# Softmax steps of equal width in a fused adaLN, attention and expert kernel: key blocks 7 and 1, 6 and 2, 5 and 3 share a score bank

## The reference

```python
h = layernorm(x) * (1 + ca) + sa
# attention: 16 heads of size 8, rotary embedding (the odd half of each pair becomes 0), causal
scores = where(causal, Q @ K^T / sqrt(8), -1e10);  y = softmax(scores) @ V
x = x + ga * (y @ Wo^T + bo)
h = layernorm(x) * (1 + cb) + sb
# experts: h @ Wm + bm is cut into 8 slices of 16; each slice takes its best 2 of 16 experts,
# gelu(t @ W1[e] + b1[e]) @ W2[e] + b2[e], weighted by the softmax over the 16 logits
x = x + gb * (experts(h) @ Wo2 + bo2)
```

## Time and profile before

| what | us |
|---|---|
| time, median of 3 runs (lowest, highest) | 398.37 (398.05, 399.06) |
| time of the profiled execution | 399.35 |
| its span | 397.5 |
| TensorE busy | 339.4 (85%) |
| VectorE busy | 287.7 (72%) |
| ScalarE busy | 256.8 (65%) |
| GpSimd busy | 134.2 (34%) |
| ScalarE exponentials and Gelus (L770), 225 instructions | 198.5 |

### The profile page before, as it was taken

How to read it: one execution, slowest core, us unless ns; L and a number is a source line. 1 busy time by engine, 2 the same in 40 slices (tenths; PEclk the granted TensorE clock), 3 DMA queues, 4 the chain that set the end, 5 groups by cost and what they waited for, 6 DMA issues and landing times.

```text
span 397.5 us, 7269 instructions
## 1 busy us (share of the span) xinstructions
PE 339.4 (85%) x2637; PEld 158.0 (40%) x2668; DVE 287.7 (72%) x590; ACT 256.8 (65%) x297; POOL 134.2 (34%) x175
## 2 busy tenths in 40 slices
PE   3659687888798599988998899988899898879996
PEld 3425244545464344433644444433554323132123
DVE  5879868997889957787489677876569546973334
ACT  7570443535178658874558878864567997968981
POOL 6246207201302604672110624742204025532500
PEclk9957789999999979999999999999999999999999
DMA  7334123200026045540116155530123255815550
GB/s 272 94 68 77 41 43 54 42 1 3 4 49 98 17 123 133 143 102 7 31 37 101 54 137 133 148 62 3 30 39 42 82 137 144 125 47 138 151 135 26
DMA packets 27115, 31.53 MB, mean 79 GB/s; under 512 B 6780, under 2 KB 17788, under 8 KB 27068
## 3 DMA queue, kind: packets, MB, share of 16 engines
q1 hardware_dynamic: 23372, 28.57, 31.2%
q0 software_dynamic: 3456, 2.39, 2.9%
q10 hardware_dynamic: 252, 0.11, 0.2%
HBM read 3.57 MB, written 1.05 MB: 12 GB/s over the span
## 4 chain that ended last, share of the span: by engine, by line
PE 55%; DVE 21%; issue 8%; ACT 6%; DMA 4%; POOL 3%; SPq 2%; DVEq 0%; ACTq 0%; POOLq 0%
PE misc L1294 18%; PE acc L1294 18%; PE big L1294 17%; DVE mx L1032 8%; ACT ring L770 5%; PE misc L1316 2%; DMA block<-qk_turned 1%; DMA tstack<-tp 1%; SPq L517 1%; DMA cc<-in_pack_c 1%; SPq L492 1%; POOL block L446 1%; POOL gm L670 1%; DVE xn L976 1%; DVE gm L1152 1%
## 5 line engine op out<-in xcount | busy, mean ns | idle before, releaser
L770 ACT ACTIVATE ring<-big 128x1024 f32<-128x1024 f32 (+2 forms) x225 | 198.5, 928 | 94.5 <-PE big L1294 93.3
L1032 DVE TENSOR_REDUCE mx<-misc 128x1 f32<-128x512 f32 (+7 forms) x155 | 87.9, 588 | 25.1 <-PE misc L1294 23.1
L1294 PE MATMUL acc<-ring,cb 128*32 128x512 f32 x512 | 68.3, 609 | 1.5 <-DVE gm L1152 1.5
L1294 PE MATMUL big<-dense,block 128*128 128x448 bf16 (+7 forms) x249 | 54.2, 317 | 5.8 <-ACT ring L770 5.6
L1294 PE MATMUL big<-tstack,w1s 128*128 128x512 bf16 x178 | 53.0, 387 | 4.8 <-ACT ring L770 3.1
L1294 PE MATMUL misc<-dense,block 128*128 128x320 bf16 (+7 forms) x167 | 42.6, 318 | 8.7 <-DVE mx L1032 8.3
L1152 DVE SCALAR_TENSOR_TENSOR gm<-acc,cb,gm 128x512 f32<-128x512 f32 (+1 forms) x41 | 30.0, 733 | 24.5 <-PE acc L1294 19.4
L446 POOL DMA_DIRECT2D block<-qk_turned x66 | 39.4, 601 | 21.6 <-DMA tstack<-tp 20.7
L1294 PEld LDWEIGHTS big<-dense,block 128*128 128x128 bf16 x256 | 30.8, 149 | 30.7 <-ACT ring L770 16.0
L1294 PE MATMUL acc<-ring,vals 128*32 128x64 f32 (+7 forms) x512 | 40.1, 414 | 0.4
L1294 PEld LDWEIGHTS misc<-dense,block 128*128 128x128 bf16 x170 | 21.0, 150 | 48.3 <-DVE mx L1032 39.2
(11 more groups left out here) (163 smaller groups left out, 459.9 us busy)
## 6 DMA issues: line engine op xcount, KB each, us to landing
gm<-wT SPq DMA_DIRECT2D x64, 256.0 KB
dense<-qk SPq DMA_DIRECT2D x42, 64.0 KB
tstack<-tp SPq DMA_DIRECT2D x18, 128.0 KB, 4.4
block<-qk_turned POOLq DMA_DIRECT2D x66, 32.0 KB, 3.2
xs<-in_x SPq DMA_DIRECT2D x4, 256.0 KB, 8.0
ca<-in_pack_a SPq DMA_DIRECT2D x1, 769.0 KB, 7.7
out<-lg SPq DMA_DIRECT2D x3, 256.0 KB, 2.3
dense<-tp SPq DMA_DIRECT2D x6, 128.0 KB, 8.9
```

The source lines that it names most:

```text
L770: act.activation(dst, src, func, scale=scale).then_inc(s["ring_read"], 1)
L1032: dve.tensor_reduce(mx[:, g, k:k + n, blk], src, AX.X, ALU.max).then_inc(s["misc_read"], 1)
L1294: return pe.matmul(dst, lhsT, rhs, start=start, stop=stop)
```

## The change

The key blocks are taken in five steps: 0; 7 and 1; 6 and 2; 5 and 3; 4. In a step of two blocks one bank holds both blocks of one pair, 64 + 448 or 128 + 384 or 192 + 320 = 512 columns, and one masking matmul serves both diagonals. A group has 9 units instead of 12, each of exactly 1024 columns, so each exponential takes 128x1024. A step is weighed once the scores of the step two later are issued, one step at a time. 18 units per softmax are no multiple of the ring's 8 slots, so slots are counted from the start of the program. The points to which other work is tied move with it: on TensorE `turn_residual`, `tokens`, `logits`, `sums_out`; on ScalarE the three turns to units 8, 9, 10, the sums to 14, the logits' exponential to 15; in softmax 0 the woven work of VectorE. The loops of `softmax` on TensorE (L1415) change as `slots` does below.

```diff
--- before.py
+++ after.py
@@ -77,10 +77,22 @@
              for n in [min(GP, T // (BLK * (s + 1)))] for k in range(0, GP, n)]
 
 
-SCORE_UNITS = [(s, 2 * k, 2, 1) for s in range(4) for k in range(2)] + [
-    (4, 0, GP, 2), (5, 0, GP, 2), (6, 0, GP, GP), (7, 0, GP, GP)]
+SOFT_STEPS = [(0,), (7, 1), (6, 2), (5, 3), (4,)]
+NSS = len(SOFT_STEPS)
+
+
+def banks_of(step):
+
+    if len(step) == 1 and T - BLK * step[0] == T // 2:
+        return [[(k + j, step[0], j * T // 2) for j in range(2)] for k in range(0, GP, 2)]
+    return [[(k, blk, sum(T - BLK * x for x in step[:j])) for j, blk in enumerate(step)] for k in range(GP)]
+
+
+SCORE_UNITS = [(i, banks_of(step)[k:k + 2]) for i, step in enumerate(SOFT_STEPS) for k in range(0, len(banks_of(step)), 2)]
 NU = len(SCORE_UNITS)
-TURN_AT, SUM_AT, ROUTE_AT = (11, 12, 13), 18, 20
+HOME = {(k, blk): (u, T * bank + at) for u, (_, banks) in enumerate(SCORE_UNITS)
+        for bank, items in enumerate(banks) for k, blk, at in items}
+TURN_AT, SUM_AT, ROUTE_AT = (8, 9, 10), 14, 15
 EARLY = 4
 
 SHARED = NB - 1
...
@@ -125,12 +137,11 @@
     order = [("early", k) for k in range(2)]
     late = []
     for g in range(NG):
-        for blk in range(NS):
-            order += [("scores", g, u) for u in range(NU) if SCORE_UNITS[u][0] == blk and (g or u >= EARLY)]
-            if len(late) == 2:
-                order += late
-                late = []
-            late.append(("weigh", g, blk))
+        for i in range(NSS):
+            order += [("scores", g, u) for u in range(NU) if SCORE_UNITS[u][0] == i and (g or u >= EARLY)]
+            late.append(("weigh", g, i))
+            if len(late) > 2:
+                order.append(late.pop(0))
     return order
 
 
@@ -139,9 +150,8 @@
     if slot[0] == "early":
         return sum(columns_of(("scores", 0, u)) for u in range(EARLY // 2 * slot[1], EARLY // 2 * (slot[1] + 1)))
     if slot[0] == "scores":
-        blk, _, n, _ = SCORE_UNITS[slot[2]]
-        return n * (T - BLK * blk)
-    return 4 * (T - BLK * slot[2])
+        return 2 * T
+    return GP * sum(T - BLK * blk for blk in SOFT_STEPS[slot[2]])
 
 
 def woven():
@@ -181,7 +191,7 @@
     return uses, banks, previous, [last[1], last[3]]
 
 
-FOLD_AT, CUT_AT = [12, 15], [18, 21, 24, 27]
+FOLD_AT, CUT_AT = [8, 10], [12, 14, 16, 18]
 OPENING, OPENING_BANK, OPENING_PREVIOUS, LAST_IN_ACC = opening()
 
 
...
@@ -784,15 +794,13 @@
                 for u in range(SOFT):
                     if u in between:
                         between[u]()
-                    blk, _, n, per = SCORE_UNITS[u % NU]
-                    w = per * (T - BLK * blk)
-                    src = big[:, 2 * (u % 2):2 * (u % 2) + n // per, 0:w]
-                    dst = ring[:, u % RING, 0:w * (n // per)].rearrange("p (k w) -> p k w", w=w)
+                    src = big[:, 2 * (u % 2):2 * (u % 2) + 2, :]
+                    dst = ring[:, (phase[0] + u) % RING, :].rearrange("p (k w) -> p k w", k=2)
                     transform("softmax", phase, u, src, dst, ACT.Exp, SCALE)
 
             def take_sums(phase, groups=range(NG)):
                 for g in groups:
-                    wait_consumed(act, phase, NS * g + NS - 1)
+                    wait_consumed(act, phase, NSS * g + NSS - 1)
                     act.copy(sums[g][:, :], acc[:, g, :]).then_inc(s["acc_read"], 1)
 
             def route(here):
@@ -816,7 +824,7 @@
                     if u in between:
                         between[u]()
                     src = big[:, 2 * (u % 2):2 * (u % 2) + 2, :]
-                    dst = ring[:, u % RING, :].rearrange("p (k w) -> p k w", k=2)
+                    dst = ring[:, (phase[0] + u) % RING, :].rearrange("p (k w) -> p k w", k=2)
                     if b == NB - 1 and u == EXPERT - 1:
                         for k in range(2):
                             transform("experts", phase, u, src[:, k], dst[:, k], ACT.Gelu, 1.0)
...
@@ -1367,34 +1375,33 @@
             def scores(m, phase, u):
 
                 g = u // NU
-                blk, k0, n, per = SCORE_UNITS[u % NU]
-                w, at = T - BLK * blk, BLK * blk
                 pe.wait_ge(s["ring_read"], phase[0] + u + 1)
-                for bk in range(n // per):
-                    dst = big[:, 2 * (u % 2) + bk, 0:per * w]
-                    for j in range(per):
-                        p = GP * g + k0 + per * bk + j
-                        matmul(dst[:, w * j:w * j + w], blocks(k_block_of[m], p, blk), q_dense_of[m][:, p, at:T], start=(j == 0), stop=False)
-                    diagonals = dst.rearrange("p (n w) -> p n w", w=w)[:, :, 0:BLK]
+                for bank, items in enumerate(SCORE_UNITS[u % NU][1]):
+                    dst = big[:, 2 * (u % 2) + bank, :]
+                    for j, (k, blk, at) in enumerate(items):
+                        p, w = GP * g + k, T - BLK * blk
+                        matmul(dst[:, at:at + w], blocks(k_block_of[m], p, blk), q_dense_of[m][:, p, BLK * blk:T], start=(j == 0), stop=False)
+                    n, apart = len(items), items[-1][2] or BLK
+                    diagonals = dst[:, 0:n * apart].rearrange("p (n w) -> p n w", w=apart)[:, :, 0:BLK]
                     ins = matmul(diagonals, identb[:, :],
-                                 earlier_query[:, :].unsqueeze(1).to_broadcast([P, per, BLK]), start=False)
+                                 earlier_query[:, :].unsqueeze(1).to_broadcast([P, n, BLK]), start=False)
                 ins.then_inc(s["ring_filled"], 1)
 
-            def weigh(m, phase, g, blk):
-
-                units = [u for u in range(NU) if SCORE_UNITS[u][0] == blk]
-                pe.wait_ge(s["ring_read"], phase[0] + g * NU + units[-1] + 1 + CREDIT["ring_read"])
-                w = T - BLK * blk
-                if g == 0 and blk == 0 and m < len(LAST_IN_ACC):
+            def weigh(m, phase, g, i):
+
+                last = max(u for u in range(NU) if SCORE_UNITS[u][0] == i)
+                pe.wait_ge(s["ring_read"], phase[0] + g * NU + last + 1 + CREDIT["ring_read"])
+                if g == 0 and i == 0 and m < len(LAST_IN_ACC):
                     pe.wait_ge(s["misc_read"], LAST_IN_ACC[m] + 1 + CREDIT["misc_read"])
-                if blk == 0 and phase[2]:
+                if i == 0 and phase[2]:
                     pe.wait_ge(s["acc_read"], NG * m)
                     wait_taken(pe, m - 1, g - 2)
-                for k in range(GP):
-                    u = next(x for x in units if SCORE_UNITS[x][1] <= k < SCORE_UNITS[x][1] + SCORE_UNITS[x][2])
-                    at = (k - SCORE_UNITS[u][1]) * w
-                    ins = matmul(acc[VW * k:VW * k + VW, g, BLK * blk:T], vals[:, GP * g + k, blk, :],
-                                 ring[:, (g * NU + u) % RING, at:at + w], start=(blk == 0), stop=(blk == NS - 1))
+                for blk in SOFT_STEPS[i]:
+                    for k in range(GP):
+                        u, at = HOME[k, blk]
+                        ins = matmul(acc[VW * k:VW * k + VW, g, BLK * blk:T], vals[:, GP * g + k, blk, :],
+                                     ring[:, (phase[0] + g * NU + u) % RING, at:at + T - BLK * blk],
+                                     start=(i == 0), stop=(i == NSS - 1))
                 ins.then_inc(s["consumed"], 1)
 
             def sums_out(here, m, g):
...
@@ -1487,7 +1493,7 @@
                 wait_taken(pe, b, n - 2)
                 for e in range(EH):
                     ins = matmul(acc[HR * e:HR * e + HR, n % 2, :], w2[:, EH * half + e, :],
-                                 ring[:, (u0 + e) % RING, T * k:T * k + T])
+                                 ring[:, (phase[0] + u0 + e) % RING, T * k:T * k + T])
                 ins.then_inc(s["consumed"], 1)
 
             def combine(here, k, half, part="", cols=slice(0, T)):
@@ -1636,16 +1642,16 @@
 
                 softmax(b + 1, softmax_at(None, b), {
                     ("scores", 0, EARLY): first_links, ("scores", 0, EARLY + 1): lambda: project(here),
-                    (0, 5): lambda: turn_residual(here, 2 * b + 3),
-                    (0, 6): lambda: tokens(here), ("scores", 1, 1): lambda: logits(here),
-                    (1, 5): lambda: sums_out(here, b + 1, 0)})
+                    (0, 4): lambda: turn_residual(here, 2 * b + 3),
+                    (1, 0): lambda: tokens(here), ("scores", 1, 3): lambda: logits(here),
+                    (1, 3): lambda: sums_out(here, b + 1, 0)})
                 experts(here, experts_at(b), NG * b + 2 * NG, ahead=True, next_sums=b + 1)
             here = ("late", NB - 2)
             turn_output(here)
             softmax(NB - 1, softmax_at(NB - 1), {
-                ("scores", 0, EARLY): lambda: project_out(here), (0, 6): lambda: turn_residual(here, 2 * NB - 2),
-                ("scores", 1, 0): lambda: tokens(here), (1, 0): lambda: logits(here),
-                (1, 5): lambda: sums_out(here, NB - 1, 0)})
```

(38 more changed lines are left out.)

## The result

The changed kernel takes 399.74 us (median of 20 runs, 398.66 to 403.27), the one before 398.28 in the same session (20 runs). The ratio is 1.0044, 95% interval 1.0029 to 1.0059: slower by 1.2 to 2.3 us. The profiled execution took 400.1 us, with a span of 398.2 against 397.5 before.

What follows compares the result with a forecast made beforehand. TensorE, with over half the chain of waits, was taken as the bound, VectorE in softmax 0. Terms -0.5 + 0.75 - 1.05 - 0.7 + 1.7 = +0.2 us gave 398.6 us on the median's scale, range 395.3 to 400.9.

Steps and rivals of the forecast that it cites:

- (a): ScalarE's exponentials and Gelus: 201 records instead of 225, all 1024 wide but for the last unit's two halves.
- (e): End of softmax 0: VectorE's wait for the values above 1.9 us.
- (b): `tokens` after the last maximum: about 1.35 us later in softmax 2, 0.75 later in softmax 1, 0.65 earlier in softmax 3.
- (c): TensorE waiting 2 to 3.5 us before `routed` in experts 1 and 2, Gelu's table load beside the last weighing.
- Softmax 0, -0.5: Softmax 0: VectorE stays the bound, its small idle times shrink, its values wait grows; -0.5 us, bounds -1.5 and +1.5.
- Softmax 1, +0.75: Softmax 1 and handover to experts 0: later `tokens` delays the SyncE-GpSimd chain whole; +0.75 us, bounds 0 and +1.5.
- Softmax 2, -1.05: Softmax 2 and handover to experts 1: `tokens` later, but waits for ScalarE go; -1.05 us, bounds -2 and +1.35.
- Softmax 3, -0.7: Softmax 3: `tokens` and the chain through `route` start earlier, so `routed` does too; -0.7 us, bounds -1.5 and +0.5.
- The clock, +1.7: Before experts 2: TensorE's 3.4 us idling brings one fall to half clock; +1.7 us, bounds 0 and 2.5.
- two falls: The wait before experts 1 also brings a clock fall; 400.3 us, up to 400.9; chance 0.21.
- `route` does not bind: Softmax 2 and 3 gain TensorE's saved waits whole, 2.0 us each, softmax 1's tokens not late; 394 us, chance 0.12.

Runs made afterwards that it cites:

- experiment 4: VectorE's routing without the order among equal second-best values: on the changed kernel 393.58 us, ratio to before 0.9892; on the kernel before 397.17 us, ratio 0.9979.

## Why the prediction was right or wrong

The time fell inside the range, 1.1 us above the forecast. It is clear of noise on the slower side, to which I had given 0.27, the least of the three. The main mechanism was right: ScalarE's gain is worth nothing by itself, TensorE's saved waits stop at VectorE's route, and one long wait brings a fall of the clock. That the total came out this near is partly luck: softmax 1 and the count of falls were too low, the price of the fall was too high.

- **Signs (a) to (e)** came, but for sizes in (b) and (c): 201 exponentials and Gelus; tokens +1.39 in softmax 2 (said 1.35) and 0.64 earlier in softmax 3 (said 0.65), but +1.12 in softmax 1 (said 0.75); waits of 2.51 and 3.71 us before `routed` (said 2.3 and 3.4, and at most 3.5); half clock behind the latter; 2.10 us before the values. The experts' stage that holds no fall kept its length (A1 to Z1 39.71).
- **Softmax 0, -0.5**: too large. The first two profiles show -0.94, but with the clock at half speed until 50.0 instead of 52.2 us. Over five profiles with the old steps V lies at 92.96 on average, over seven with the new ones at 92.81: -0.15, less than its own scatter of 1 us.
- **Softmax 1, +0.75**: +1.12 (V to T1 23.97 with no fall, against 22.85). The late parts of the queries don't play in there, but the same extra wait for tokens (2.41 instead of 1.30) does, and its +1.35 of softmax 2 should have been the centre.
- **Softmax 2, -1.05**: -0.74. **Softmax 3, -0.7**: -0.68.
- **The clock, +1.7**: the fall came, at 1.03 us. I had priced it by the thin stretch up to the first product; there it is free, since that product waits for a DMA, and what is paid is the backlog behind it. For experts 0 the same method was too low (2.7).
- **The step that was off** is the count of falls. I counted the one place where the change makes a wait longest and took all else as equal. These terms alone give -0.15 + 1.12 - 0.74 - 0.68 + 1.03 = +0.6 us; measured are 1.6 on the means. Time at half clock elsewhere has the size of the missing us: the changed kernel has 8.5 us more of it on average, of which the fall before experts 2 is 3.4, and the other 5.1 at 0.22 are 1.1 us. That is an estimate from averages. The profiles do not show where the 5.1 lie. Of the changed kernel's two, both fell at 101 us (V to T1 24.78 and 24.93 against 23.97 without a fall) and one before `routed` in experts 1 (0.74); of the kernel before's two, neither fell at 101, but one at 212.6 (1.6). Over all profiles the fall at 101 stands in five of eight with the new steps and in two of five with the old, and in those two it lasts 6.9 us instead of 3.4 and costs 1.9 us (V to T1 24.79 and 24.80 against 22.85), in the five 0.6 to 1.0. So neither place is shown to cost the changed kernel more.
- **The rival "two falls"** had about the size (400.3) and half of the mechanism. It took the length of the idle time to decide, and the runs do not bear that out: the clock fell at a wait of 1.40 us and did not behind one of 2.51.
- **`route` does not bind** is refuted by experiment 4.

What stays open is why the clock falls at 101 us in one execution and not in another with the same wait ahead (1.40 us in both kernels), and in which stages the missing microsecond is lost.

## What to carry to other kernels

When a change takes waits away from the busiest engine, look for the next chain that this engine must meet, and move that chain's first instruction forward in the same edit: here one matmul, one burst of weighing too late, turned a gain of 1.8 us into a loss of as much. Many short waits joined into a long one can cost more than their sum, as they put the clock at risk (here 1.0 us on top of the wait). The fillers that paid here began within 0.7 us of the last real work, in a bank that was free there, and ended before the data; the one that began after 2.97 us of idling and ended 4 us behind the data did not. Compare stretches between fixed instructions, not totals: here most repeat within 0.1 us, while the total moves by 1% with the clock.

## What the hardware showed that I had not expected

- Where the clock falls is not fixed for a kernel. Waits of 2.47 and 2.51 us before the same instruction ended with and without a fall, waits of 1.40 us at 101 us likewise, and a busy stretch behind a wait of 1.01 us fell as well. In its advice on throughput drops, the Trainium skill (TensorE: Matmul & The Clock Gate, section "Why this matters for your kernels") warns of long gaps between bursts. Of the five falls behind 100 us in the changed kernel's second profile two (139.0 and 309.7) go with waits of 4.46 and 3.71 us; the other three go with waits of 1.40, 2.12 and 2.47 us and show that keeping the waits shorter is no safeguard.
- A microsecond at half clock costs 0.22 us on average over the kernel before (a slope over 75 runs, not a controlled test; that most of it lies beside waits for VectorE or DMAs is the likely reason), but 0.3 before experts 2 (1.03 for 3.4) and 0.4 in experts 0 (2.7 for 6.8).
